# A mixture of experts that gathers its slots by token number and finishes each tile as it comes

## The reference

```python
logits = x @ router_w
expert_idx = jnp.argmax(logits, axis=-1)
score = jax.nn.sigmoid(jnp.max(logits, axis=-1))
xs = x * score[:, None]
for e in range(8):
    m = (expert_idx == e)[:, None]
    xe = jnp.where(m, xs, 0.0)
    h = silu(xe @ gate_w[e]) * (xe @ up_w[e])
    out = out + jnp.where(m, h @ down_w[e], 0.0)
shared = silu(x @ shared_gate_w) * (x @ shared_up_w) @ shared_down_w
...
x = _layernorm(x + out + shared)
```

## Time and profile before

| what | us |
|---|---|
| median of 3 runs | 3572.8 (3567.86 to 3587.13) |
| the profiled execution | 3576.2 |
| its span in the trace | 3574.4 |
| TensorE busy in the span | 3033.0 (85%) |
| VectorE, ScalarE, GpSimd busy | 1690.6, 1241.0, 599.8 |
| the mixture stage in the span | about 2979 to 3574.4 |

### The profile page before, as it was taken

One profiled execution on the slowest core, in us unless ns is written; L12 is line 12 of the kernel. 1 busy time (PEld: TensorE's weight loads), 2 busy tenths in 40 slices (PEclk: granted clock), 3 DMA queues, 4 the chain that ended last, 5 costly groups with the idle time before them and its releaser, 6 DMA issues. The chain is left out here.

```text
span 3574.4 us, 48594 instructions
## 1 busy us (share of the span) xinstructions
PE 3033.0 (85%) x16338; PEld 2034.3 (57%) x16339; DVE 1690.6 (47%) x3232; ACT 1241.0 (35%) x3220; POOL 599.8 (17%) x647
## 2 busy tenths in 40 slices
PE   6999869888873999999688885999999996999894
PEld 4676523233322777777555554888888885444441
DVE  5666656776643111221166663666666663111113
ACT  2333326556550111111044442555655552111110
POOL 1000031332223000000100002333333332200002
PEclk9999969889876999999899997999999998999997
DMA  1000076567614000000100002111211106201323
GB/s 65 19 23 24 13 166 135 123 155 145 148 62 136 13 13 12 13 24 7 45 13 23 23 18 77 48 48 59 83 60 48 47 24 244 106 0 35 129 94 115
DMA packets 127374, 235.40 MB, mean 66 GB/s; under 512 B 15384, under 2 KB 27928, under 8 KB 127216
## 3 DMA queue, kind: packets, MB, share of 16 engines
q1 hardware_dynamic: 106560, 190.20, 18.9%
q0 software_dynamic: 12528, 32.40, 2.7%
q10 hardware_dynamic: 8128, 10.67, 1.0%
HBM read 161.55 MB, written 71.14 MB: 65 GB/s over the span
## 5 line engine op out<-in xcount | busy, mean ns | idle before, releaser
L1297 DVE TENSOR_REDUCE x_minus_max<-banks 128x2 f32<-128x1024 f32 x256 | 308.1, 1222 | 155.4 <-PE banks L1363 153.6
L1245 ACT ACTIVATE x_probs<-banks 128x512 f32<-128x512 f32 x512 | 272.3, 598 | 145.2 <-PE banks L1381 137.0
L481 ACT ACTIVATE a_probs<-banks,a_minus_max 128x128 f32<-128x128 f32 (+1 forms) x512 | 208.6, 425 | 146.5 <-DVE a_minus_max L564 145.0
L1381 PEld LDWEIGHTS banks<-x_stacked_q,x_stacked_k 53*128 53x128 f32 x512 | 64.3, 201 | 206.9 <-issue 159.7
L1381 PE MATMUL banks<-x_stacked_q,x_stacked_k 53*128 53x512 f32 x512 | 161.4, 530 | 23.1 <-ACT x_probs L1245 19.4
L2118 POOL TENSOR_TENSOR x_probs<-x_probs,x_inverse 128x512 f32<-128x512 f32 x128 | 133.1, 1040 | 274.4 <-DVE x_inverse L2327 274.4
L2852 DVE TENSOR_TENSOR m_h<-banks,m_silu 128x512 f32<-128x512 f32 x39 | 27.0, 692 | 319.7 <-PE banks L2968 166.5
L2182 ACT ACTIVATE x_probs<-banks,x_minus_max,x_rroot 128x256 f32<-128x256 f32 x256 | 142.9, 566 | 91.4 <-DVE x_minus_max L2293 91.4
L564 DVE TENSOR_REDUCE a_minus_max<-banks 128x2 f32<-128x512 f32 (+1 forms) x192 | 131.8, 687 | 82.3 <-PE banks L714 61.8
L1690 DVE TENSOR_TENSOR f_hT<-banks,f_silu 128x256 f32<-128x256 f32 (+1 forms) x88 | 37.3, 424 | 280.7 <-ACT f_silu L1616 280.7
L1363 PE MATMUL banks<-x_stacked_k,x_stacked_q 51*128 51x512 f32 x512 | 135.8, 481 | 38.6 <-DVE x_minus_max L1297 13.0
(11 more groups left out here) (372 smaller groups left out, 7746.5 us busy)
## 6 DMA issues: line engine op xcount, KB each, us to landing
x_parts_dram<-x_parts SPq DMA_DIRECT2D x16, 1024.0 KB, 5.9
x_x<-x_after SPq DMA_DIRECT2D x24, 512.0 KB, 4.2
x_stacked_k<-x_parts_dram SPq DMA_DIRECT2D x96, 128.0 KB
x_stacked_q<-x_parts_dram SPq DMA_DIRECT2D x96, 128.0 KB
x_after<-a_z SPq DMA_DIRECT2D x16, 512.0 KB, 2.8
x_z<-x_after SPq DMA_DIRECT2D x16, 512.0 KB, 7.3
x_heads_dram<-x_heads_out SPq DMA_DIRECT2D x32, 256.0 KB
x_after<-x_z SPq DMA_DIRECT2D x16, 512.0 KB, 3.4
```

Source lines behind the costliest of these rows:

```text
L481: ins = act.activation(probs[:, n % 3, i * width:(i + 1) * width], psum[uses.bank(use)][:, i * width:(i + 1) * width], ACT.Exp, bias=minus ...
L1245: act.activation(probs[:, n % 8, :], psum[at.bank(f"exp{n}")], ACT.Exp, scale=SCALE)\
L1297: dve.tensor_reduce(minus_max[:, c % 2, h % 4:h % 4 + 2, t], at.pair(use), AX.X, ALU.max, negate=True)\
L1381: ins = pe.matmul(psum[at.bank(use)], stacked[1][u][rows, h // 2, s * P:(s + 1) * P].bitcast(F32R), stacked[0][u][rows, h // 2, :].bitcast ...
```

## The change

Only `mixture` changes, with one more constant input.

- x comes in eight pieces of two tiles into a ring, and TensorE transposes it from there without a copy; all transposes are kept (`xT_all`) and the shared tiles use them. The router products follow the transposes by two tiles.
- Tile 0's gate product stands ahead of the two counting products, and its up, gate 1 and up 1 ahead of anything that needs the routing.
- Nothing of x is scattered. GpSimd scatters 16 bytes for each token (its number and score) to `slot_meta`, which the constant input has filled with numbers beyond 2047, and loads that back. VectorE turns it into `source_row` (unused rows: 2047) and `target_row` before tile 6.
- The shared tiles add x (loaded again by ScalarE's queue) and go to the DRAM tensor `base`.
- For each slot GpSimd gathers the rows of x and of `base` by number, four slots ahead. The score enters as a scale of silu and of h.
- Each slot is finished at once: VectorE adds `base` to y, takes statistics, waits for GpSimd's power, normalises; GpSimd scatters the rows to the result by number, and skips those beyond 2047.
- TensorE's order in a tile is gate, transposes of the next slot's x, up, the reading of the next slot's four numbers, down of the tile before, transposes of h. All loops are written out.

```diff
+            def load_chunk(k):
+                if k >= len(x_loaded):
+                    sp.wait_ge(first_full, (k - len(x_loaded) + 1) * CHUNK)
+                at = k % len(x_loaded) * CHUNK
+                sp.dma_start(rows[:, at:at + CHUNK, :], src[:, k * CHUNK:(k + 1) * CHUNK, :])\
+                    .then_inc(x_loaded[k % len(x_loaded)], 16)
...
+            for k in range(4):
+                load_chunk(k)
+            load_shared(0, "sg")
+            for k in range(4, CHUNKS):
+                load_chunk(k)
+            load_shared(1, "su")
+            load_shared(2, "sd")
...
-                sp.dma_start(dst[:, k * GROUP:(k + 1) * GROUP, :], rows[:, k * GROUP:(k + 1) * GROUP, :]).then_inc(stored, 16)
+            for k in range(OUT_RING):
+                sp.wait_ge(stored[k], 16 * len(range(k, NS, OUT_RING)))
...
+            pool.wait_ge(pads_stored, 16)
+            pool.wait_ge(routed, ROUTED)
             for t in range(NT):
...
-                pool.indirect_dma_start(out=slot_x, out_offset=bass.IndirectOffsetOnAxis(ap=index[:, t:t + 1], axis=0),
-                                        in_=scaled_x[:, t % 2, :], in_offset=None).then_inc(scattered[t % 2], 16)
...
-            pool.dma_start(rows[:, NT:NT + NS, :], slot_x.rearrange("(g p) d -> p g d", p=P)).then_inc(slots_loaded, 16)
...
-                pool.indirect_dma_start(out=rows[:, NT + t, :], out_offset=None, in_=slot_y,
...
+                pool.indirect_dma_start(out=slot_meta, out_offset=bass.IndirectOffsetOnAxis(ap=index[:, t:t + 1], axis=0),
+                                        in_=meta[:, t, :], in_offset=None).then_inc(scattered, 16)
+            pool.wait_ge(scattered, 16 * NT)
+            pool.dma_start(slots[:, :, :], slot_meta.rearrange("(g p) m -> p g m", p=P)).then_inc(slots_loaded, 16)
...
+            def gather_x(s):
+                if s >= RING:
+                    pool.wait_ge(xT_full, s - RING + 1)
+                pool.indirect_dma_start(out=x_in[s % RING], out_offset=None, in_=src_rows,
+                                        in_offset=bass.IndirectOffsetOnAxis(ap=source_row[:, s:s + 1], axis=0))\
+                    .then_inc(x_gathered[s % RING], 16)
...
+            def gather_base(s):
+                if s >= RING:
+                    pool.wait_ge(y_ready, NT + s - RING + 1)
+                pool.indirect_dma_start(out=base_in[s % RING], out_offset=None, in_=base,
+                                        in_offset=bass.IndirectOffsetOnAxis(ap=source_row[:, s:s + 1], axis=0))\
+                    .then_inc(base_gathered[s % RING], 16)
...
+            pool.wait_ge(first_full, NT)
+            pool.wait_ge(ids_ready, 2)
+            for s in range(RING):
+                gather_x(s)
+            for k in range(RING):
+                pool.wait_ge(base_stored[k], 16 * (NT // RING))
+            for s in range(RING):
+                gather_base(s)
+            for s in range(NS):
+                pool.wait_ge(moved, 2 * s + 2)
+                pool.tensor_tensor(rstd[:, s:s + 1], vareps[:, s:s + 1], core.minus_half[:, 0:1], ALU.pow).then_inc(rstd_ready, 1)
+                if s + RING < NS:
+                    gather_x(s + RING)
+                    gather_base(s + RING)
+                pool.wait_ge(out_ready, s + 1)
+                pool.indirect_dma_start(out=dst_rows, out_offset=bass.IndirectOffsetOnAxis(ap=target_row[:, s:s + 1], axis=0),
+                                        in_=z[:, s % OUT_RING, :], in_offset=None, bounds_check=ALL_ROWS - 1,
+                                        oob_is_err=False).then_inc(stored[s % OUT_RING], 16)
...
+            act.dma_start(slot_meta, weights["pads"]).then_inc(pads_stored, 16)
+            for t in range(NT):
+                act.wait_ge(first_full, t + 1)
+                act.copy(xT_all[:, t], psum[t % 4].rearrange("p (c t) -> p c t", c=KC)).then_inc(first_ready, 1)
...
+            for t in range(3):
+                load_shared_x(t)
...
+            for t in range(LAST + 1):
+                u, s = t % 2, t - NT
                 act.wait_ge(gate_full, t + 1)
+                if t >= 2:
                     act.wait_ge(h_ready, t - 1)
+                if s == 0:
+                    act.wait_ge(slots_loaded, 16)
+                act.activation(silu[:, u, :], psum[GATE + u], ACT.Silu, scale=slots[:, s, 1:2] if s >= 0 else 1.0)\
+                    .then_inc(silu_ready, 1)
+                if 0 <= s + 1 < NS:
+                    act.wait_ge(xT_full, s + 2)
+                    act.wait_ge(up_full, t)
+                    act.copy(xT[:, (s + 1) % 2], psum[XT + 1 - u].rearrange("p (c t) -> p c t", c=KC)).then_inc(xT_ready, 1)
                 act.wait_ge(hT_full, t + 1)
...
+                if t >= 2:
                     act.wait_ge(y_full, t - 1)
                 act.copy(hT[:, u], psum[XT + u].rearrange("p (c t) -> p c t", c=KC)).then_inc(hT_ready, 1)
...
+                if 1 <= t <= NT:
+                    act.wait_ge(y_ready, t)
+                    act.dma_start(base[(t - 1) * P:t * P, :], base_in[(t - 1) % RING]).then_inc(base_stored[(t - 1) % RING], 16)
+                if t >= 2 and t + 1 < NT:
+                    load_shared_x(t + 1)
...
+            def give_y(t):
+                u, s, k = t % 2, t - NT, t % RING
                 dve.wait_ge(y_full, t + 1)
...
+                if s < 0:
+                    dve.wait_ge(shared_x_loaded[k], 16 * (t // RING + 1))
+                    dve.tensor_tensor(base_in[k], psum[DOWN + u], base_in[k], ALU.add).then_inc(y_ready, 1)
+                    return
+                dve.wait_ge(base_gathered[k], 16 * (s // RING + 1))
+                if s >= OUT_RING:
+                    dve.wait_ge(stored[s % OUT_RING], 16 * (s // OUT_RING))
+                row = z[:, s % OUT_RING, :]
+                dve.tensor_tensor(row, psum[DOWN + u], base_in[k], ALU.add).then_inc(y_ready, 1)
+                dve.wait_ge(y_ready, t + 1)
+                dve.bn_stats(stats[:, s, :], row).then_inc(z_stats, 1)
+                dve.wait_ge(z_stats, s + 1)
+                dve.bn_aggr(moments[:, s, :], stats[:, s, :]).then_inc(moved, 1)
+                dve.wait_ge(moved, 2 * s + 1)
+                dve.tensor_scalar(vareps[:, s:s + 1], moments[:, s, 1:2], EPS, None, ALU.add).then_inc(moved, 1)
+                dve.wait_ge(rstd_ready, s + 1)
+                dve.tensor_scalar(row, row, moments[:, s, 0:1], rstd[:, s:s + 1], ALU.subtract, ALU.mult).then_inc(out_ready, 1)
+            for t in range(LAST + 1):
+                u, s = t % 2, t - NT
+                if t == IDS_AT:
+                    dve.wait_ge(slots_loaded, 16)
+                    dve.tensor_scalar(source_row[:, :], slots[:, :, 0], float(ALL_ROWS - 1), None, ALU.min).then_inc(ids_ready, 1)
+                    dve.tensor_copy(target_row[:, :], slots[:, :, 0]).then_inc(ids_ready, 1)
                 dve.wait_ge(silu_ready, t + 1)
                 dve.wait_ge(up_full, t + 1)
+                if t >= 2:
                     dve.wait_ge(hT_full, t - 1)
...
+                if s < 0:
+                    dve.tensor_tensor(h[:, u, :], psum[UP + u], silu[:, u, :], ALU.mult).then_inc(h_ready, 1)
+                else:
+                    dve.scalar_tensor_tensor(out=h[:, u, :], in0=psum[UP + u], scalar=slots[:, s, 1:2], in1=silu[:, u, :],
+                                             op0=ALU.mult, op1=ALU.mult).then_inc(h_ready, 1)
+                if t >= 1:
+                    give_y(t - 1)
+            give_y(LAST)
...
+            def first_transposes(t):
+                if t % CHUNK == 0:
+                    k = t // CHUNK
+                    pe.wait_ge(x_loaded[k % len(x_loaded)], 16 * (k // len(x_loaded) + 1))
+                if t >= 4:
+                    pe.wait_ge(first_ready, t - 3)
                 for c in range(KC):
+                    ins = pe.transpose(psum[t % 4][:, c * P:(c + 1) * P], rows[:, t % (2 * RING), c * P:(c + 1) * P], core.ident[:, :])
+                ins.then_inc(first_full, 1)
...
+            for t in range(NT + 2):
+                if t < NT:
+                    first_transposes(t)
+                if t >= 2:
+                    first_logits(t - 2)
...
+            def transpose_x(s):
+                t = NT + s
+                pe.wait_ge(x_gathered[s % RING], 16 * (s // RING + 1))
+                pe.wait_ge(hT_ready, t - 1)
+                for c in range(KC):
+                    ins = pe.transpose(psum[XT + t % 2][:, c * P:(c + 1) * P], x_in[s % RING][:, c * P:(c + 1) * P], core.ident[:, :])
+                ins.then_inc(xT_full, 1)
...
+            def down(t, buffer):
+                u = t % 2
...
                 pe.wait_ge(hT_ready, t + 1)
+                if t >= 2:
+                    pe.wait_ge(y_ready, t - 1)
+                product(DOWN + u, hT[:, u], buffer, 2, y_full)
...
+            def transpose_h(t):
+                pe.wait_ge(h_ready, t + 1)
+                if t >= 2:
```

(33 more changed lines are left out.)

328 lines of the change are left out of this document (89 added, 239 removed).

## The result

The changed kernel takes 3463.3 us (median of 4 runs, 3458.9 to 3469.7) against 3572.8 us: ratio 0.9688, 95% interval 0.9663 to 0.9713. Forecast were 3451 us and a range of 3438 to 3495, so it is 109.5 us faster where 122 were forecast. The profiled execution took 3461.7 us, with a span of 3459.6 us.

A forecast was written before the change was run, and what follows sets the result against it. TensorE was taken to bound the tiles, with the last 50 us idle for it. Last down product ends at 3442.0, plus 1.5 stall, 0.3 and 8.5 tail: 3452.3 us span, 3454.1 profiled, forecast 3451 us median; range 3438 to 3495.

The forecast's parts named there:

- 1 and 2, start and routing: Start of the mixture stage: TensorE starts at 2983.9 us, 10.3 us routing chain hidden beside first products; about 27 us gained.
- 3, shared tiles: Shared tiles: x transposes and their pause gone, 10.80 us a tile against 12.21; about 20 us gained.
- 4, slots: Slots: x transposes behind gate, four number reads covered, 11.29 us a slot; about 33 us gained together with weights.
- the point from which VectorE's finish would cost: Slots: VectorE's finish, about 4.2 us from the end of down, makes h late only if over 7.8 us.
- 5, weights: Weight loads in the slots: a set takes 12.6 us with 11.8 us available; stall 1.5 us in all, ends 0 and 10.
- 6, tail: End of the kernel: 8.5 us from the last add on to the end, against 50.6 before; about 42 us gained.
- E: Rival, slots: GpSimd becomes the bound; at 4.6 us for each indirect issue 143 us more, 3594 us; chance 0.04.
- The sign that the forecast is wrong "if any stage before 2979 us moves": Untouched stages ahead of the mixture stage: they keep their time, and any movement there shows the forecast wrong.
- A: Rival, slots: gathers of unused rows meet weight bursts, stalls of 2 to 7 us in six slots; 3463 to 3493; chance 0.13.
- B: Rival, slots: number reads happen only when up has run, 22 x 3.0 = 66 us; 3517 us; chance 0.04.
- D: Rival, slots: VectorE's finish takes over 7.8 us, h comes late; at 10.8 us, 3 us a slot, 3517; chance 0.04.
- C: Rival, tile 6: token numbers load late, costing beyond 39 us; at three times 19.7, 20 us lost: 3471; chance 0.04.

The follow-up runs named there:

- xt_first: Changed kernel with the transposes of the next slot's x moved ahead of the gate product; median 3486.1 us, ratio 0.9751, slot pitch 12.13 us.
- five_reads: Changed kernel with five number reads, then the next slot's x transposes, ahead of gate, as in the kernel before; median 3486.7 us, ratio 0.9742.
- fewer_dmas: Changed kernel without gathers of base from the fifth slot on and without scatters except those of slots 21 and 22; 3459.4 us in one run.
- write_late: Changed kernel with all powers, normalisations and scatters moved behind the last tile; median 3499.7 us, ratio 0.9774.

## Why the prediction was right, and where its sizes were off

The direction, the order of size and, but for the closing of GpSimd, the mechanisms held. By stage the gains were 28.4 us for start and routing (27 forecast), 20.2 for the shared tiles (20), 31.0 for slots and weights (33) and 38.4 for the tail (42), 118.0 in all. That VectorE's last add came within 0.3 us of the forecast is partly luck: 2.1 us gained up to slot 0 and 2.4 us gained by a shorter pitch stand against 4.0 us more for weights and 0.8 us at the last down product.

- **1 and 2, start and routing.** Right within 1.1 us. The undoing gave 12.7 us for the routing alone, 10.1 of it the chain and the rest the clock behind the idle time. No run undoes the other 15.7 us; 5.6 of them are TensorE's earlier start.
- **3, shared tiles.** Right: 10.74 us against 10.80, though no run puts the old order back into a shared tile; xt_first prices it in the slots. Nothing waits; ScalarE's two added issues cost nothing.
- **4, slots.** Right: 11.18 against 11.29, and the cover holds: with the finish at 9.2 us or the reads at the tile's start a slot loses at most 0.25 us. Of the 1.45 us from the old pitch of 12.63, the place of the x transposes is 0.95; the other 0.50, by the distances under five_reads, lies with the reads, as the prediction says, but not by its numbers: five reads were to take 3.75 us and end behind the copy of hT, and in the slot of the earlier trace rows they end at 3382.3, 0.2 us ahead of it, with another 0.5 us until the transposes of x. Wrong was the point from which VectorE's finish would cost: I set the time when h is due at the end of up, but the down product stands between up and the transposes that need h. A term was missing at the end: the last down product has no other work ahead of it and waits 0.76 us for hT. And the base rows of slot 0, forecast 3.5 us ahead of their need, came 4.0 us behind it:

```profile
L2880 DVE TENSOR_TENSOR m_z<-banks,m_rows x23: 691/692/693, 3204.1 to 3447.4; 128x512 f32<-128x512 f32 x23
...
  DMA m_rows<-base_rows,m_source_row: 4.0, 1
```

  Nobody waited for VectorE there, so it cost nothing.
- **5, weights.** The step that was mis-sized by 4.0 us: 5.5 against 1.5. A set took not 10.6 or 12.6 us but, from its first issue to the gate that it released, 12.4 before slot 10 (3280.92 to 3293.32) and 14.0 before slot 20 (3393.78 to 3407.81), and the clock added 1.8 us. Beside fewer gathers and scatters (fewer_dmas) it took 12.8 before slot 20. The sum of 5.5 lies inside the bounds of 0 and 10.
- **6, tail.** Mis-sized by 3.7 us, 12.2 against 8.5: I ended the sum with the landing of the last scatter (2.1 us after its issue) and never asked what GpSimd still owes for 86 DMAs, 7.1 us. Writing each slot at once instead of behind the last tile is worth 32.7 us by write_late. The row of the kernel before was there (4.47 us), but hidden by the result's store.
- **From span to median.** Of the 12.3 us between 3451.0 and 3463.3, 3.2 came from untouched work ahead of the stage and 4.1 from the stage; and I put the median 3.4 us (3576.2 less 3572.8) under the profiled execution, as before, where it came 1.5 us above it, which makes the other 4.9.
- **The chances.** 3463.3 us lies at the very end of the 3440 to 3463 that had 0.70. All but E and half of the rest add up to 0.955, where the text has 0.94 and 0.02 for the same time. The sign that the forecast is wrong "if any stage before 2979 us moves" was badly set: by 3.2 us these stages moved, and in the other kernels by up to 15 us, with no line of them changed.
- **The rivals.** A came about in kind, not in size: late weights, in two slots of its six, from their burst. B falls: the reads run while gate does, and at the tile's start, where the down product covers most of them, they cost 0.25 us. D falls at 9.2 us, and with E by write_late. C falls, nothing waited for the token numbers:

```profile
m_slots<-slot_meta POOLq DMA_DIRECT2D x1, 46.0 KB, 4.9
```

  2944 pieces of 16 bytes landed in 4.9 us, at 3050.5 us and far under the bound of 19.7; VectorE takes them up at 3073.1. The Trainium skill ("DMA: Bandwidth & Descriptors", "Specifications") says that transfers under 512 B do a read-modify-write; whatever that cost here is inside these 4.9 us.

## What to carry to other kernels

Undo a merged change one place at a time: moving four transposes across one product was worth 0.95 us a tile, because of whose copy they stood behind, and moving the number reads alone 0.25 us. Ask for a buffer's parts when each comes free, not when the last does; a burst at the last moment costs its length, and the clock may fall behind the wait. When GpSimd's indirect DMAs end a kernel, count them: the end comes when GpSimd has closed, not when the last row has landed.
